# Merging 104 candidates instead of 192 in a top-32 scan, with its test on GpSimd, fills on VectorE and new orders

## The chip, the cores and the metric

The kernel runs on one core of a Trainium2 chip. The metric is the time of one execution in microseconds of the device, the median of several runs. Three runs of the kernel before gave 5827.73, 5835.18 and 5836.25 us.

## The reference

Input x is 16 batches of 256 rows of 128 columns; a context has 1601 rows for each batch. Four stages follow each other, each added to x through a gate: cross attention with 16 heads of 8 columns, a top-2 mixture of eight experts, a cross attention that keeps the 32 best keys of each query, and self attention with a second mixture. The change is in the third:

```
def _L1_xattn_ref(query, key, value, Wq, bq, Wk, bk, Wv, bv, Wo, bo):
    HID, NH, TOPK = (128, 16, 32)
    ...
    scores = jnp.einsum('bhqd,bhkd->bhqk', q, k) / SCALE
    top_scores, top_idx = jax.lax.top_k(scores, eff_k)
    w = jax.nn.softmax(top_scores, axis=-1)
    top_v = jnp.take_along_axis(v[:, :, None, :, :], top_idx[..., None], axis=3)
    out = jnp.einsum('bhqk,bhqkd->bhqd', w, top_v)
```

## The kernel before

Work is cut into batches (16) and groups of four heads (64, four to a batch). A step has a name and a key; each engine has a list of names (`ORDER`), which stands for one round of about a batch, and a table of lags (`LAG`) that says by how many steps each name stays behind. The list is gone through 21 times, so steps of some five batches are under way at once. Every engine does its list strictly in order; semaphores hold it back where data is missing.

The steps the text speaks of:

- `x_in`, `ctx_in`, `ln_stats`, `ln_aggr`, `ln_pow` (GpSimd, L1277), `ln_scale` (L1019), `ln_turn`, `w_k`, `w_q`: a batch is loaded, normalized, multiplied by weights. `split` (GpSimd, L1288 to L1295) cuts projected keys and queries into three bf16 parts, SP stores them in HBM (L1359) and loads them again, stacked, as `k_scan` and `k_att`.
- First scan (layer 0): `n0` multiplies scores on TensorE (L586) into one of two `score` banks, `n0_max` reduces them on VectorE into `part` (L1031).
- Second scan (layer 1): `c1` on TensorE (L601) fills one of the two `wide` buffers, `c1_out` on ScalarE (L886) copies them to `s`, four buffers of 128 queries x 1601 scores. Such a tile is one head's 128 queries; there are 512, 32 to a batch. `rank` on VectorE takes tile n and, between its searches, merges tile n - 1: it comes in four parts. The finding part (L933) takes the eight best of each of 24 pieces of 66 or 67 columns. The merging part (L949 to L978) takes the best 32 of the 192 candidates: four searches of eight, and between them three replacements of what was found by a very small number.
- The result is wrong only where a piece held more than seven of the best 32. So `eighth` is the largest of the 24 eighth values (L961), and `flag` tells whether it beats the 32nd (L978). For each pair of tiles `flag` on TensorE sums these flags over the queries (L768), `check` on VectorE reduces the sum (L1067), reads it into a register and, if it isn't zero, searches both tiles again over all 1601 columns (L1079, L1082). `c1_out` reuses a buffer of `s` only after the check of the tile four back. `least` (L1095 to L1106) makes the threshold of each query from its best and its 32nd value.
- Attention: `s_0`, `s_1`, `s_z` fill a `wide` buffer (L627, L639), ScalarE takes the exponential (L905), `pv` multiplies by the values (L673). For layer 1 ScalarE first marks what lies below the threshold (`cut`, L895), and `cut_add` (L649) adds it in place. `u_turn`, `o_norm`, `o_turn`, `o_proj`, `x_add` end a layer.
- All products that aren't in `wide`, `score` or `att` share one bank, `small`, which each user claims from the one before.

At the start GpSimd fills every buffer whose rows beyond the stacked ones must be zero or one (L1257 to L1265), and its first `ln_pow` and `split` come behind that.

## Time and profile before

| what | value |
|---|---|
| median of three runs | 5835.18 us |
| the profiled execution | 5828.82 us |
| its span, first to last instruction | 5826.2 us |
| TensorE, VectorE, ScalarE, GpSimd busy | 4721, 4724, 4048, 866 us |
| mean granted TensorE clock | 0.923 |
| HBM traffic | 56 GB/s over the span |

Busy times are the union of an engine's instructions. Of a matmul the end is modelled, so a busy TensorE is not one at its peak. VectorE's instructions overlap: each is recorded longer than the distance to the next one's start. In a row of a wait the engine that is named last held the other back.

### The profile page before, as it was taken

What the parts mean: (1) busy time and instruction counts of PE and PEld (TensorE: products, weight loads), DVE (VectorE), ACT (ScalarE), POOL (GpSimd) and SP (SyncE); (2) the same over time, 40 slices, a digit from 0 to 9 for tenths busy, and PEclk for the clock granted to TensorE, in tenths of its full rate; (3) what the DMA queues carried; (4) which work ended last, traced back from release to release, by engine and by line L of the source; (5) the groups of instructions that cost most, each with busy time, mean ns of one, the idle gap of its engine ahead of it and who ended that gap; (6) DMA issues with size and microseconds to landing.
All of it is one profiled execution on the core that took longest, in us unless ns stands there. A gap on an engine that the chain in (4) does not pass through costs nothing. (4 is left out here: it accounts for less than half of the span.)

```text
span 5826.2 us, 109134 instructions
## 1 busy us (share of the span) xinstructions
PE 4721.2 (81%) x34222; PEld 2250.7 (39%) x34758; DVE 4723.8 (81%) x23731; ACT 4047.7 (69%) x5196; POOL 866.3 (15%) x1650
## 2 busy tenths in 40 slices
PE   4878679898787989788788988887898788988666
PEld 1434234343343435334343534434353343434222
DVE  3468888888888888888888888888888888877773
ACT  1447667878586787768668787876878587786654
POOL 4211111111110111111111111111111111010000
PEclk7889889999899999999999999999999899998777
DMA  4322221312222222222212222221222222121110
GB/s 108 81 64 56 58 57 50 75 46 73 50 62 54 54 66 52 68 60 55 61 48 71 57 68 64 60 71 40 68 52 70 54 51 56 49 51 26 28 28 18
DMA packets 356330, 332.19 MB, mean 57 GB/s; under 512 B 102073, under 2 KB 313148, under 8 KB 355710
## 3 DMA queue, kind: packets, MB, share of 16 engines
q1 hardware_dynamic: 355710, 324.84, 22.6%
q8 instruction: 277, 4.54, 0.3%
q14 instruction: 343, 2.81, 0.2%
HBM read 217.54 MB, written 107.13 MB: 56 GB/s over the span
## 5 line engine op out<-in xcount | busy, mean ns | idle before, releaser
L933 DVE MAX8 cand<-s 128x8 f32<-128x67 f32 (+1 forms) x12288 | 2084.9, 216 | 235.3 <-ACT s L886 139.1
L905 ACT ACTIVATE prob<-wide 128x1024 f32<-128x1024 f32 (+1 forms) x1792 | 1765.7, 1024 | 380.9 <-PE wide L627 169.5
L1031 DVE TENSOR_REDUCE part<-score 128x1 f32<-128x512 f32 (+1 forms) x2048 | 1122.3, 565 | 429.2 <-PE score L586 286.2
L627 PE MATMUL wide<-q,k_att 128*128 128x256 bf16 (+1 forms) x6656 | 1027.8, 282 | 251.3 <-ACT prob L905 149.4
L673 PE MATMUL att<-prob,v 128*9 128x256 f32 (+1 forms) x14336 | 1118.2, 391 | 48.8 <-ACT prob L905 16.0
L886 ACT ACTIVATE s<-wide 128x1024 f32<-128x1024 f32 (+1 forms) x1024 | 827.4, 840 | 421.0 <-PE wide L601 290.0
L895 ACT ACTIVATE below<-wide 128x1024 bf16<-128x1024 f32 (+1 forms) x832 | 835.4, 1027 | 117.4 <-PE wide L627 110.7
L627 PEld LDWEIGHTS wide<-q,k_att 128*128 128x128 bf16 (+1 forms) x6656 | 563.0, 101 | 763.9 <-ACT prob L905 393.5
L586 PE MATMUL score<-k_scan,q 128*128 128x512 bf16 (+1 forms) x1724 | 560.6, 342 | 338.7 <-DVE part L1031 295.1
L601 PE MATMUL wide<-k_scan,q 128*128 128x512 bf16 (+1 forms) x1981 | 528.6, 356 | 71.3 <-ACT prob L905 33.6
L649 PE MATMUL wide<-below,minus_ident 128*128 128x512 bf16 (+1 forms) x1519 | 469.1, 392 | 101.6 <-ACT below L895 71.0
L586 PEld LDWEIGHTS score<-k_scan,q 128*128 128x128 bf16 x2048 | 199.0, 99 | 713.6 <-DVE part L1031 380.4
L673 PEld LDWEIGHTS att<-prob,v 128*9 128x9 f32 (+1 forms) x14336 | 227.1, 89 | 505.7 <-issue 395.3
L1304 POOL CAST shift<-minus 8x128 bf16<-8x128 f32 x192 | 54.0, 281 | 2114.8 <-issue 1886.0
L866 ACT ACTIVATE hid<-wide,b 128x256 f32<-128x256 f32 x512 | 200.5, 474 | 216.7 <-PE wide L715 216.5
L1288 POOL CAST split_b<-split_f 128x256 bf16<-128x256 f32 (+2 forms) x192 | 91.6, 477 | 1541.0 <-issue 860.3
L728 PE MATMUL small<-w,hid 128*128 128x128 f32 x2048 | 298.5, 289 | 0.0
L601 PEld LDWEIGHTS wide<-k_scan,q 128*128 128x128 bf16 x2048 | 153.2, 100 | 344.3 <-ACT s L886 125.8
L715 PE MATMUL wide<-v_xnT,w 128*128 128x256 f32 x1024 | 263.6, 403 | 23.0 <-ACT hid L866 17.0
L728 PEld LDWEIGHTS small<-w,hid 128*128 128x128 f32 x2048 | 249.5, 192 | 31.1 <-issue 0.4
L649 PEld LDWEIGHTS wide<-below,minus_ident 128*128 128x128 bf16 (+1 forms) x1664 | 113.9, 100 | 327.3 <-ACT below L895 275.9
L1277 POOL TENSOR_TENSOR rstd<-rstd,half 128x2 f32<-128x2 f32 x64 | 44.3, 693 | 1203.0 <-DVE rstd L1010 1201.8
(165 smaller groups left out, 5744.8 us busy)
## 6 DMA issues: line engine op xcount, KB each, us to landing
k_scan<-k_stack SPq DMA_DIRECT2D x512, 150.1 KB, 2.7
k_stack<-split_b SPq DMA_DIRECT2D x576, 128.0 KB, 2.5
k_att<-k_stack SPq DMA_DIRECT2D x384, 192.0 KB, 3.3
ctxT<-in_ctx_dram SPq DMA_DIRECT2D x32, 800.5 KB, 4.6
q_stack<-split_b SPq DMA_DIRECT2D x192, 64.0 KB, 2.1
q<-q_stack SPq DMA_DIRECT2D x128, 96.0 KB
self_stack<-split_b SPq DMA_DIRECT2D x192, 64.0 KB, 2.1
k_self<-self_stack SPq DMA_DIRECT2D x64, 96.0 KB
```

What stands on the lines that cost most here:

```text
L586: tensor.matmul(score[i % 2][:, 0:wd], m.q[0][g % QBUF[0]][:, hh, qt * P:(qt + 1) * P], m.k_scan[0][(HG * g + hh) % 2][:, a0:a0 + wd], sta ...
L601: r = tensor.matmul(ps[:, n0:n1], m.q[1][g % QBUF[1]][:, hh, qt * P:(qt + 1) * P], m.k_scan[1][(HG * g + hh) % 2][:, a0 + n0:a0 + n1], sta ...
L627: r = tensor.matmul(ps[0:kc, j * S:(j + 1) * S], m.k_att[kn % 3][:, j, c0:c0 + kc], rows[:, j, :], start=(j % 2 == 0), stop=(l == 0), skip ...
L649: r = tensor.matmul(ps[0:kc, x:x + BANK], m.minus_ident[0:kc, 0:kc], m.below[n % 2][0:kc, x:x + BANK], start=False, stop=True, skip_group_ ...
L673: r = tensor.matmul(att[32 * j:32 * j + HD + 1, 0:S], v[0:kc, c, j0 * HG + j, :], m.prob[n % 3][0:kc, j * S:(j + 1) * S], start=(c == 0), ...
L715: r = tensor.matmul(ps[:, k * S:(k + 1) * S], m.w_1[:, e, k * P:(k + 1) * P], m.xnT["v"][:, :], start=True, stop=True)
L728: r = tensor.matmul(ps[:, t * D:(t + 1) * D], hid[:, k, t * P:(t + 1) * P], m.w_2[:, e, k, :], start=False, stop=(k == PT - 1))
L886: scalar.activation(m.s[tile % 4][:, a0:a0 + wd], ps[:, 0:wd], ACT.Copy).then_inc(sem["wide_done"], 1)
L895: scalar.activation(m.below[n % 2][0:kc, :], ps[0:kc, :], ACT.Relu, scale=-STEEP).then_inc(sem["cut_done"], 1)
L905: scalar.activation(pr[0:kc, :], ps[0:kc, :], ACT.Exp, scale=SCALE).then_inc(sem["wide_done"], 1)
L933: i = vector.max(cand[:, c, :], s[:, KCUT[c]:KCUT[c + 1]])
L1031: vector.tensor_reduce(m.part[:, QT * hh + qt, c:c + 1], score[i % 2][:, 0:wd], AX.X, ALU.max).then_inc(sem["score_max"], 1)
```

## The change

It has five parts.

1. A buffer of candidates is now 8 + 192 columns wide and ordered by rank: first eight free columns, then the first values of all 24 pieces, then the second, and so on. Columns 8 to 103 are the four best of each piece, 104 to 199 the lower four. One search takes the best eight of the lower 96 into the free columns; the merge's searches and replacements run over columns 0 to 103. There are three such buffers and not two.
2. The result may be wrong where an eighth value of a piece, or the eighth of the lower ones, beats the 32nd. Both are compared on GpSimd, as a step `mark` with two operations per tile that write 25 flags in bf16; the product of `flag` has 50 columns, and `check` reduces 50.
3. In a part of `rank` three finding searches stand before each of two merging instructions, where two stood before each of up to three.
4. The fills of zeros and ones are done by VectorE before its first step.
5. `ORDER` and `LAG` of all engines are other tables.

```diff
-        "rank": 482, "n0_max": 257, "n0_all": 9, "o_norm.1": 17, "ln_scale.w": 1, "check": 61, "least": 16,
+        "rank": 491, "n0_max": 257, "n0_all": 9, "check": 62, "o_norm.1": 17, "least": 16, "x_add.1": 5,
...
-        m.cand = [sb(f"cand{n}", [P, KC, 8]) for n in range(2)]
-        m.left = sb("left", [P, KC, 8])
+        m.cand = [sb(f"cand{n}", [P, 8 + 8 * KC]) for n in range(3)]
+        m.left = sb("left", [P, 8 + 4 * KC])
-        m.eighth, m.flag = sb("eighth", [P, 1]), [sb(f"flag{n}", [P, QT]) for n in range(2)]
+        m.flag = sb("flag", [P, QT, KC + 1], BF16)
...
-                        q.wait_ge(ranked, 9 * (scan_tile(g, 2 * pair + 1) + 1))
-                        tensor.matmul(ps[0:1, 0:QT], m.ones_col[:, :], m.flag[(HG * g + pair) % 2][:, :],
+                        q.wait_ge(sem["marked"], after("mark", scan_tile(g, 2 * pair + 1)))
+                        tensor.matmul(ps[0:1, 0:QT * (KC + 1)], m.ones_col[:, :], flat(m.flag),
...
-                        if tile >= 2 and c == 0:
-                            q.wait_ge(ranked, 9 * (tile - 1))
-                        i = vector.max(cand[:, c, :], s[:, KCUT[c]:KCUT[c + 1]])
+                        if tile >= 3 and c == 0:
+                            q.wait_ge(ranked, 8 * (tile - 2))
+                            q.wait_ge(sem["marked"], after("mark", tile - 3))
+                        i = vector.max(cand[:, :, c], s[:, KCUT[c]:KCUT[c + 1]])
...
+                    upper, lower, left = cand[:, 0:8 + 4 * KC], cand[:, 8 + 4 * KC:], m.left[:, :]
+                    n, done = tile % 8, 8 * tile
                     best = [ends[:, n, 0, :], m.top[:, 0, :], m.top[:, 1, :], ends[:, n, 1, :]]
                     if part == 0:
                         q.wait_ge(cand_done, 4 * (tile + 1))
-                        q.wait_ge(ranked, done)
+                        vector.max(cand[:, 0:8], lower).then_inc(ranked, 1)
+                        yield
+                        q.wait_ge(ranked, done + 1)
                         if tile >= 16:
                             q.wait_ge(sem["least_done"], after("least", tile // 8 - 2))
+                        vector.max(best[0], upper).then_inc(ranked, 1)
+                        yield
                     else:
+                        q.wait_ge(ranked, done + 2 * part)
+                        vector.match_replace(left, best[part - 1], upper if part == 1 else left, NEG).then_inc(ranked, 1)
                         yield
+                        q.wait_ge(ranked, done + 2 * part + 1)
+                        vector.max(best[part], left).then_inc(ranked, 1)
                         yield
...
+                        for blank in (*m.q[0], *m.k_scan[0], *m.q[1], *m.k_scan[1]):
+                            vector.memset(blank[:, :] if len(blank.shape) == 2 else flat(blank), 0.0)
+                        for blank in (*m.k_att, *(x for pair in m.kq_self for x in pair)):
+                            i = vector.memset(flat(blank), 0.0)
+                        i.then_inc(blanked, 1)
+                        q.wait_ge(blanked, 1)
+                        for blank in (*m.k_att, *(x for x, _ in m.kq_self)):
+                            i = vector.memset(blank[32:ROWX, :, :], 1.0)
+                        i.then_inc(blanked, 1)
...
-                        for n in range(9):
-                            if n % 3 < 2:
+                        for n in range(8):
+                            if n % 4 < 3:
                                 next(finds, None)
                             else:
                                 next(merges, None)
...
-                        vector.tensor_reduce(m.many[:, :], small[0:1, 0:QT], AX.X, ALU.max).then_inc(sem["checked"], 1)
+                        vector.tensor_reduce(m.many[:, :], small[0:1, 0:QT * (KC + 1)], AX.X, ALU.max).then_inc(sem["checked"], 1)
...
+                    elif name == "mark":
+                        tile, = key
+                        cand = m.cand[tile % 3]
+                        flags, kth = m.flag, m.ends[tile // 8 % 2][:, tile % 8, 1, 7:8]
+                        q.wait_ge(ranked, 8 * (tile + 1))
+                        if tile >= 2:
+                            q.wait_ge(sem["small_full"], after("flag", (tile - 2) // 8, (tile - 2) % 8 // QT))
+                        gpsimd.tensor_scalar(flags[:, tile % QT, 0:KC], cand[:, 8 + 7 * KC:], kth, None,
+                                             ALU.is_gt).then_inc(sem["marked"], 1)
+                        gpsimd.tensor_scalar(flags[:, tile % QT, KC:KC + 1], cand[:, 7:8], kth, None,
+                                             ALU.is_gt).then_inc(sem["marked"], 1)
```

How instructions stand now, at three places. First VectorE in the middle of the program, from the last search of the merge of a pair's second tile (`ends<-left`) to that pair's check (`many`); the pair is the second of group 34. Before:

```order
L973 MAX ends<-left 128x8
L933 MAX cand<-s 128x8 x2
L978 TENSOR_TENSOR flag<-eighth,ends 128x1
...
L1216 SCALAR_TENSOR_TENSOR v_acc<-small,v_one,v_acc 128x128 x2
L933 MAX cand<-s 128x8 x2
L956 MAX top<-left 128x8
L933 MAX cand<-s 128x8 x2
L959 MATCH_REPLACE left<-top,left 128x192
L933 MAX cand<-s 128x8 x2
L961 TENSOR_REDUCE eighth<-cand 128x1
L1031 TENSOR_REDUCE part<-score 128x1 x2
L1067 TENSOR_REDUCE many<-small 1x1
```

And now:

```order
L1028 TENSOR_REDUCE part<-score 128x1
L1044 TENSOR_REDUCE mx<-score 128x2
L942 MAX cand<-s 128x8 x3
L964 MATCH_REPLACE left<-top,left 128x104
L942 MAX cand<-s 128x8 x3
L967 MAX ends<-left 128x8
L1064 TENSOR_REDUCE many<-small 1x1
L1066 TENSOR_LOAD many
```

The check has moved from two parts of a scan behind the merge to directly behind it. Over the middle 128 checks 2.8 parts of `rank` and 7.4 steps in all stood between the two in the mean; now it is 0.9 and 2.7, and in 8 of the 128 nothing stands between.

Second VectorE at the start of the program. Before:

```order
L984 MEMSET u 128x256
L1000 BN_STATS stats<-x 128x6 x2
L1007 BN_AGGR mv<-stats 128x2 x2
L1010 TENSOR_SCALAR rstd<-mv 128x2
L1019 TENSOR_SCALAR xn<-x,mv,rstd 128x128 x2
```

And now, where the widths are those of 32-bit words for the zeros of all but `k_scan`:

```order
L974 MEMSET q_2 128x512
L974 MEMSET k_scan_0 128x1601
L974 MEMSET k_scan_1 128x1601
L976 MEMSET k_att 128x1024 x3
L976 MEMSET k_self 128x512
L976 MEMSET q_self 128x512
L976 MEMSET k_self 128x512
L976 MEMSET q_self 128x512
L980 MEMSET k_att 19x2048 x3
L980 MEMSET k_self 19x1024 x2
L997 BN_STATS stats<-x 128x6 x2
```

All in all 22,276 columns of fills stand ahead of the first statistics.

Third GpSimd in the middle of the program, around the split of the last 65 columns of a projection. Before:

```order
L1288 CAST split_b<-split_f 128x65
L1290 TENSOR_TENSOR split_f<-split_f,split_b 128x65
L1293 CAST split_b<-split_f 128x65
L1295 TENSOR_TENSOR split_b<-split_f,split_b 128x65
L1304 CAST shift<-minus 8x128
L1306 TENSOR_TENSOR res<-minus,shift 8x128
```

And now:

```order
L1284 CAST split_b<-split_f 128x65
L1286 TENSOR_TENSOR split_f<-split_f,split_b 128x65
L1289 CAST split_b<-split_f 128x65
L1291 TENSOR_TENSOR split_b<-split_f,split_b 128x65
L1271 TENSOR_SCALAR flag<-cand,ends 128x24
L1273 TENSOR_SCALAR flag<-cand,ends 128x1
```

The marks stand in the same queue as splits and shifts and wait for whatever is in front.

## Rows read from the trace of the kernel before

**Rows 1.** The page, part 1: busy us, share of the span and instructions.
```profile
PE 4721.2 (81%) x34222; PEld 2250.7 (39%) x34758; DVE 4723.8 (81%) x23731; ACT 4047.7 (69%) x5196; POOL 866.3 (15%) x1650
```
**Rows 2.** Busy time by stretch: start:end, length, engines, granted clock, DMA share, GB/s.
```profile
787.00:1077.00 290.00, 234.35 (x1697) 116.05 (x1723) 253.19 (x1200) 200.94 (x265) 49.45 (x95) 0.93 0.24 57
3472.00:3798.00 326.00, 284.77 (x2142) 137.98 (x2172) 281.05 (x1474) 252.98 (x326) 51.53 (x100) 0.98 0.25 63
5586.00:5713.00 127.00, 81.47 (x546) 28.44 (x555) 91.14 (x561) 79.64 (x95) 8.43 (x24) 0.77 0.09 20
```
**Rows 3.** The last addition into x of two neighbouring batches, with their starts.
```profile
L1153 DVE SCALAR_TENSOR_TENSOR x<-z_acc,gates,x x2: 485/486/486, 3471.8 to 3797.9; 128x256 f32<-128x256 f32 x2
```
**Rows 4.** Waits from 3472 to 3798 us: total, times, longest.
```profile
DVE part L1031 <- PE score L586: 12.9, 16, 1.4
DVE many L1067 <- PE small L768: 2.6, 4, 1.2
```
```profile
PE wide L627 <- ACT prob L905: 9.5, 21, 1.0
PE score L586 <- DVE part L1031: 5.8, 9, 1.6
```
**Rows 5.** Timeline of VectorE, merging: start, duration, line, operation, count.
```profile
658.97 0.34 DVE L949 MAX8 ends<-cand 128x8 f32<-128x192 f32 x1
659.23 0.34 DVE L933 MAX8 cand<-s 128x8 f32<-128x67 f32 x2
659.49 0.07 DVE L952 MATCH_VALUE_LOAD left<-ends,cand 128x8 f32 x1
...
661.44 0.17 DVE L961 TENSOR_REDUCE eighth<-cand 128x1 f32<-128x24 f32 x1
661.53 0.34 DVE L933 MAX8 cand<-s 128x8 f32<-128x67 f32 x2
...
663.68 0.14 DVE L978 TENSOR_TENSOR flag<-eighth,ends 128x1 f32<-128x1 f32 x1
663.74 0.34 DVE L933 MAX8 cand<-s 128x8 f32<-128x66 f32 x2
```
**Rows 6.** VectorE by form (busy us, mean ns), and the flag line (minimum, median, maximum ns).
```profile
L978 DVE TENSOR_TENSOR flag<-eighth,ends 128x1 f32<-128x1 f32 x512 | 87.3, 170 | 0.0
L1082 DVE MAX8 ends<-s 128x8 f32<-128x1601 f32 x32 | 58.5, 1829 | 5.9 <-DVE many L1067 5.1
L1067 DVE TENSOR_REDUCE many<-small 1x1 int32<-1x2 f32 x256 | 35.6, 139 | 76.9 <-PE small L768 75.9
```
```profile
L978 DVE TENSOR_TENSOR flag<-eighth,ends x512: 132/143/1143, 382.9 to 5704.2; 128x1 f32<-128x1 f32 x171
```
**Rows 7.** GpSimd by form: one operation of a split, a small cast, the smallest fill.
```profile
L1295 POOL TENSOR_TENSOR split_b<-split_f,split_b 128x512 bf16<-128x512 f32 x96 | 111.2, 1159 | 7.7
L1309 POOL CAST shift<-res 8x128 bf16<-8x128 f32 x192 | 54.0, 281 | 12.3
L1444 POOL MEMSET const-float32-1.0<- 128x1 f32 x1 | 0.1, 98 | 0.0
```
**Rows 8.** The start: timeline rows of each engine, and busy times and DMA from 35 to 40 us.
```profile
0.86 0.27 DVE L984 MEMSET u<- 128x256 f32 x1 [0.86 <-PEq L1444]
44.35 1.95 DVE L1019 TENSOR_SCALAR xn<-x,mv,rstd 128x128 f32<-128x128 f32 x2 [23.83 <-POOL rstd L1277]
```
```profile
27.96 0.51 SPq L1324 DMA_DIRECT2D w<-in_L_ffn_W_dram  x1
48.15 7.71 SPq L1359 DMA_DIRECT2D k_stack<-split_b  x12
```
```profile
48.74 0.58 PE L541 MATMUL small<-w_oT,b_v 128*1 128x128 f32 x2
...
74.30 1.04 PE L586 MATMUL score<-k_scan,q 128*128 128x512 bf16 x2 [19.17 <-DMA k_scan<-k_stack]
```
```profile
35.00:40.00 5.00, 0.00 (x0) 0.00 (x0) 0.00 (x0) 0.00 (x0) 4.79 (x5) 0.50 0.00 0
```

More of the change, by code:

```diff
@@ L73 @@
     v_add=("v_added", 1), z_add=("z_added", 8), b_o_add=("b_o_done", 1), zero_u=("u_zero", 1),
-    ln_pow=("pow_done", 1), split=("split_done", 4), shift=("shift_done", 4),
+    ln_pow=("pow_done", 1), mark=("marked", 2), split=("split_done", 4), shift=("shift_done", 4),
 )
@@ L139 @@
     pool="""
-        shift.0 shift.1 split.w_k.0*2 ln_pow.z split.z_qk*2 ln_pow.v split.w_q shift.0 split.w_k.0 shift.1 shift.2
-        ln_pow.u shift.2 shift.0 split.u_q shift.1 split.w_k.0 shift.2 split.w_k.1 shift.2 shift.0 split.w_k.1*3
-        shift.1 ln_pow.w""",
+        mark shift.0 split.w_k.1 mark*4 shift.1 ln_pow.z mark*2 split.z_qk*2 mark ln_pow.v mark*2 shift.0 split.w_k.0
+        mark*2 shift.2 shift.1 ln_pow.w mark*3 split.w_k.0 mark split.w_q ln_pow.u mark shift.2 shift.0 mark
@@ L143 @@
+        split.w_k.0 split.u_q mark shift.2 mark shift.1 mark split.w_k.0 mark*4 shift.2 mark shift.0 split.w_k.1
+        mark*2 shift.1 mark split.w_k.1 mark*2 split.w_k.1 mark""",
     sp="""
-        q_in.1 k_scan.1 rows_out.0 rows_in.0 ctx_in.0 k_scan.0 k_att.0 k_att.1 k_scan.0 k_scan.1 rows_out.1 k_att.1*2
-        q_in.0 rows_in.1 split_out.w_k.0*2 k_scan.0 k_scan.1 k_att.1 k_att.0 k_scan.0 k_scan.1 k_att.0
-        split_out.z_qk*2 k_att.0 q_in.1 kq_in*2 split_out.w_q k_scan.1 rows_out.0 rows_in.0 split_out.w_k.0 k_scan.0
@@ L176 @@
     pool={
-        "shift.0": 9, "shift.1": 16, "split.w_k.0": 4, "ln_pow.z": 5, "split.z_qk": 10, "ln_pow.v": 3, "split.w_q": 1,
-        "shift.2": 20, "ln_pow.u": 3, "split.u_q": 3, "split.w_k.1": 8, "ln_pow.w": 0},
-    sp={
[3 rows of a table removed]
-        "split_out.w_k.1": 8, "x_out": 5, "x_in": 0},
+        "mark": 124, "shift.0": 9, "split.w_k.1": 9, "shift.1": 16, "ln_pow.z": 5, "split.z_qk": 10, "ln_pow.v": 3,
+        "split.w_k.0": 4, "shift.2": 20, "ln_pow.w": 1, "split.w_q": 1, "ln_pow.u": 3, "split.u_q": 3},
@@ L251, in streams @@
     of("rank", "rank", [(n, part) for n in range(QT * HG * NG + 1) for part in range(4)])
+    of("mark", "mark", [(n,) for n in range(QT * HG * NG)])
     for name in ("flag", "check"):
@@ L970, in merge @@
                         yield
                     else:
-                        q.wait_ge(ranked, done + 7)
-                        vector.max(best[3], left).then_inc(ranked, 1)
+                        q.wait_ge(ranked, done + 2 * part)
+                        vector.match_replace(left, best[part - 1], upper if part == 1 else left, NEG).then_inc(ranked, 1)
                         yield
-                        q.wait_ge(ranked, done + 8)
-                        if tile >= 4:
-                            q.wait_ge(sem["small_full"], after("flag", (tile - 4) // 8, (tile - 4) % 8 // QT))
@@ L978, in merge @@
-                        vector.tensor_tensor(m.flag[tile // QT % 2][:, tile % QT:tile % QT + 1], m.eighth[:, :],
-                                             ends[:, n, 1, 7:8], ALU.is_gt).then_inc(ranked, 1)
+                        q.wait_ge(ranked, done + 2 * part + 1)
+                        vector.max(best[part], left).then_inc(ranked, 1)
                         yield
```

216 lines of the change are left out of this document (94 added, 122 removed), and 6 rows, old and new, of the table sp.

## The prediction

> **What bounds the kernel now.** I read the page's busy shares first, then the steady stretch, then who waits for whom in it. The page has TensorE and VectorE level at 81% of the span, with ScalarE at 69% and GpSimd at 15% [rows 1]. Averages over the ramp hide the stage that counts. The last addition into x of a batch tells the pace: in a batch in which no scan is repeated it comes every 326.1 us [rows 3]. In exactly that stretch TensorE is busy 284.8 us, VectorE 281.1 and ScalarE 253.0 [rows 2]: two engines level at 87%, a third at 78%. No DMA matters there (0.25 of its engines busy). So this is not one bottleneck but three engines in fixed orders that lock into each other. The wait rows say how: VectorE's largest wait is for scores of TensorE, 12.9 us, and TensorE's are for ScalarE's `prob` (9.5 us on that one row) and for VectorE's `part` (5.8) [rows 4]. VectorE is idle 326.1 - 281.1 = 45 us in a batch, TensorE 41 us.
>
> **Part 1, the merges.** An instruction's mean hides what it costs, since VectorE's instructions overlap; the step from one start to the next does not. A search of 192 candidates starts at 658.97 and the next instruction at 659.23: 0.26 us. Two searches of a 67-column piece take 659.23 to 659.49, 0.13 each [rows 5]. The slope is (259 - 130) / 125 = 1.03 ns per column, so 104 columns cost 130 + 37 x 1.03 = 168 ns, and 96 cost 160. Before, a tile has seven passes over 192 (four searches, three replacements); each falls by 91 ns, together 0.64 us. Gone are the reduction of the eighths (661.44 to 661.53, 0.09 us) and the flag's comparison (663.68 to 663.74, 0.06 us, and now and then a stall: its median is 143 ns, its mean 170 and its longest 1143 [rows 6], so some 0.03 more). New is the search of the 96 lower candidates, 0.16. Net 0.64 + 0.09 + 0.06 + 0.03 - 0.16 = 0.66 us per tile. The loads of the eight values stay. The cost of the scattered store (eight values 24 columns apart) is in no row; I take it as nothing, from a search that puts out 8 values whatever it reads, and as the bad bound 8 cycles more per search, which at 1.03 ns is 24 x 8 = 198 ns per tile, a third of the gain.
>
> The check now reduces 50 columns where it reduced 2 [rows 6]: 48 x 1.03 = 0.05 us, 16 times a batch. A batch has 32 tiles: VectorE is relieved of 32 x 0.66 - 0.8 = 20.3 us, and in 512 tiles of 325 us.
>
> **How much of that reaches the end.** TensorE's work does not change (the flag product is small either way), so its 284.8 us stay. If the whole 20.3 us arrived, the batch would be 306 us and TensorE busy 93% of it; no stretch of the trace has it above 88%. The lower bound is what TensorE's own idle time owes to VectorE: 5.8 us for `part` [rows 4] and 5.9 in five smaller rows (`xn`, `mx`, `o`), together 11.7 us. The rest of its idle time is ScalarE's, whose work stays. Between 11.7 and 20.3 I take 14, nearer to the lower end, since that already asks for 91% of TensorE. VectorE would be at 84% then, and TensorE alone is late next. I count 14 batches at this gain (the stage from 787 us has VectorE at 87% too, TensorE at 81% [rows 2]): 196 us. In the last two batches VectorE is less busy, at the end 72% [rows 2], and waits for ScalarE's copies: half of 20.3 each, 20 us.
>
> **Part 2, repeats of a scan.** A repeat is 14 passes over 1601 columns at 1.8 us, 26 us in a batch; the row has 32 first or last searches of that width, two per tile, so 16 tiles in 8 pairs [rows 6]. The new rule also repeats when the eighth of the lower candidates beats the 32nd value. I worked both rules out on the reference's inputs: the same 8 pairs of 256 are marked, and no row has more than 5 of its best 32 among the lower candidates where 8 would be needed. Cost nothing, and nothing covers for it.
>
> **Part 3, the test on GpSimd.** Two comparisons a tile, 24 columns and 1. No such row exists here. From below stands a GpSimd fill of one column, 0.1 us; from above a cast on 8 x 128 at 281 ns [rows 7]. I take 0.25 each, nearer to the cast, which also reads. That is 16 us a batch on an engine that works 51.5 of 326 us [rows 2], so its time is free. What is not free is the chain. Before, the flag came from VectorE itself; now it goes last search, semaphore, two comparisons, TensorE's product, check: 0.5 for the comparisons, some 0.4 for the product and up to 0.3 for hand-overs, 1.2 us. Between the last search of a pair and its check stood 7.4 of VectorE's steps in the mean, 2.8 of them parts of a scan; now 2.7, of them 0.9 parts. A part takes about 1.1 us, so the cover is mostly still longer than 1.2; but in one check of 16 nothing at all stands between (the first place shown under the change), and in one a single short addition. That is 1.2 + 0.8 = 2 us a batch. GpSimd does its queue in order, and a mark may stand behind a split, which is four operations and some 3.5 us, the two long ones 1.16 each [rows 7]. Behind a waiting check on VectorE stand the searches of the next tile and `n0_max`, for which TensorE's scores wait. Before, the checks waited 2.6 us a batch [rows 4], so I charge 1 us more, 16 us in all.
>
> What speaks against the move is contention. The flag comparison's own row shows it: 143 ns as a rule, 1143 at worst when GpSimd was at work [rows 6]. The Trainium skill (SBUF — State Buffer, section SBUF: two separate sides) has one pair of ports that a GpSimd operation and a VectorE operation with two SBUF inputs hold for the whole instruction, the other being blocked. By that rule 1024 more GpSimd operations block VectorE's remaining two-input steps, some 40 a batch; at 0.25 us and GpSimd's 5% more occupancy that is under 1 us a batch, and the comparison that suffered most is the one removed. The sum is the same within its range.
>
> **Part 4, the start.** GpSimd fills until 43.5 us and makes the first `rstd` behind that, and only then can VectorE scale the first x (44.35), and SP store the first split (48.15), though SP's queue was through with the weights at 28.5 and nothing lands any more from 35 on, the weights included [rows 8]. TensorE's first score follows at 74.3. Now VectorE fills: 256 columns took 272 ns [rows 8], so 1.06 ns a column; 22,300 columns (zeros written as 32-bit words where the count allows, as the built program has it) are 23.7 us, and VectorE is free at 24.6. Then come 1.8 us of statistics and the power, so the first x is scaled at 26.8, 17.6 us sooner. SP's store can come 19.6 us sooner, and the bias product that waits for all weights can come by 35 at worst against 48.7 [rows 8], 13.7 us. So 14 to 17 us, and 10 if VectorE's fills had to wait for the 7 us of fills that GpSimd keeps. I take 15. The Trainium skill (VectorE: DVE Perf Modes, section Zero memsets can be issued as uint32) gives one cycle per element, 23.2 us for the same columns; the row and the rule agree, and the widths here come from it.
>
> **Part 5, the orders.** The second scan lags 4 half-tiles more and the attention of layer 1 by 7 of 52 chunks. The last step of a batch comes five rounds after its first in both, so there are 16 + 5 = 21 rounds in both; what leaves the ramp is added at the tail; I take nothing for it, within 10 us.
>
> **Sum.** The profiled execution took 5828.8 us; 5828.8 - 196 - 20 + 16 - 15 = 5614. The median of the runs is 6 us above that execution, so 5620.
>
> **Rivals.**
> *All of it arrives* (the new order lets TensorE reach 93%): 20.3 x 16 + 15 = 340 less, 5495. For it: the part of the wait rows that names ScalarE is itself a loop through the two wide buffers, which a new order can loosen. Against it: no stretch above 88%.
> *TensorE holds at its 88%*: the batch becomes 284.8 / 0.88 = 323.6 and 14 batches give 35; with the start and 10 at the tail 5775. The wait rows of ScalarE for TensorE speak for it.
> *The test becomes the new wait, slower than before*: place, the check on VectorE. The gain without it is 231 us over 256 checks, 0.9 us each. If marks come behind splits (3.5 us) where the cover is one part and one `n0_max`, 1.7 us, each check stalls by 1.2 us more: 307 us, and the time is 5829 - 231 + 307 + 6 = 5911. It decides from 0.9 us per check. Against it: GpSimd works 16% of a batch [rows 2], so few marks should find it busy.
> *Nothing moves*: the new order loses in ScalarE's loop what VectorE gains, 5835.
>
> **How the numbers follow.** The forecast (5530 to 5700) has 0.52, all of it 0.14, TensorE holds (5700 to 5820) 0.18, nothing 0.05, the test as new wait 0.11. Faster by over 0.2% is 0.52 + 0.14 + 0.18 = 0.84, the same 0.05, slower 0.11; 0.2%, 12 us, is about what a measurement of this kernel can tell from no change. The range leaves out the slower case and the lower half of the second, 0.18 in all, and so takes in the case in which nothing moves: 5490 to 5840.
>
> **What would show it.** A batch without a repeat near 312 us, with TensorE at about 285 and VectorE at about 261 busy: right. Searches over 104 columns that start 0.168 us before the next, else part 1 is off. The first score at 57 to 64 us, else part 4. VectorE's waits of `many` for the product near 4 us a batch; 15 or more would be the slower rival. A batch of 320 or more with few check waits would be TensorE's limit. A ninth pair scanned again would make part 2 wrong.

## The result, and the profile after

The changed kernel takes 5451.2 us (median of 4, 5441.8 to 5462.4) against 5831.5 for the kernel before on the same chip: a ratio of 0.934, interval 0.933 to 0.936. It is 380 us faster. The forecast was 5620 and the range ended at 5490: the sign was right, and the size missed by nearly a factor of two (215 us of gain forecast, 380 measured). The time lies below even the rival in which everything arrives, 5495.

The page of the changed kernel, part 1 (busy us, share of the span, instructions), answers to [rows 1]:

```profile
span 5460.3 us, 110204 instructions
...
PE 4684.1 (86%) x34502; PEld 2229.0 (41%) x34502; DVE 4361.7 (80%) x23240; ACT 4036.6 (74%) x5196; POOL 1154.4 (21%) x2648
```

VectorE works 362 us less, TensorE hardly less, and the span is 366 us shorter. TensorE's share rises from 81% to 86%. The same by stretch, as in [rows 2] (start:end, length, busy us of TensorE, weight loads, VectorE, ScalarE, GpSimd, granted clock, DMA share, GB/s), for the first full stage, a batch without a repeat, and the end:

```profile
787.00:1024.00 237.00, 199.13 (x1469) 98.31 (x1469) 198.47 (x967) 172.26 (x227) 49.35 (x114) 0.92 0.21 53
3270.00:3571.00 301.00, 280.15 (x2164) 135.72 (x2156) 257.21 (x1442) 252.16 (x326) 71.56 (x164) 1.00 0.27 68
5336.00:5460.00 124.00, 79.91 (x393) 29.55 (x393) 27.40 (x87) 40.94 (x55) 12.06 (x29) 0.64 0.09 21
```

And the pace, the last addition into x of two neighbouring batches of the changed kernel, as in [rows 3]:

```profile
L1150 DVE SCALAR_TENSOR_TENSOR x<-z_acc,gates,x x2: 1262/1263/1264, 3270.3 to 3571.4; 128x256 f32<-128x256 f32 x2
```

The batch takes 301 us, where it took 326. VectorE is busy 257.2 us in it (281.1 before), ScalarE unchanged. TensorE, whose work the change leaves alone, is busy 280.2 of 301 us: 93%, with an idle time of 21 us where it had 41. A part of that is the clock: its mean grant is 1.00 in this stage where it was 0.98, and the same work takes 4.6 us less. Over the whole run the mean grant is 0.936 where it was 0.923, and TensorE's busy time falls by 37 us, so as an estimate from these busy times the clock accounts for a tenth of the 366 us at most.

The 366 us between the two profiled executions lie in three places. Up to the last addition of the first batch (1077 us before, 1024 after) 53, of which 18 are gained by the first score. In the 12 batches behind it, 1077 to 5158 before and 1024 to 4835 after, 4081 against 3811 us: 270, or 22.5 a batch. In the rest 43. Six of these 12 batches have no repeat in either kernel; they took 326.3 us in the mean before and 302.5 now.

Who waits for whom in that batch of the changed kernel (engine, what, line, who is waited for: us in total, times, longest), as in [rows 4]:

```profile
PE wide L657 <- ACT below L903: 4.0, 12, 0.5
PE wide L609 <- ACT prob L913: 2.9, 8, 0.5
PE score L594 <- DVE part L1028: 2.1, 4, 0.7
PE wide L635 <- ACT prob L913: 2.0, 6, 0.5
PE wide L635 <- ACT s L894: 1.9, 4, 0.8
```
```profile
DVE v_acc L1213 <- PE small L736: 9.6, 5, 4.3
DVE part L1028 <- DVEq L1082: 8.5, 11, 0.9
DVE part L1028 <- PE score L594: 6.3, 12, 1.1
DVE many L1064 <- PE small L776: 6.0, 7, 2.5
DVE cand L942 <- ACT s L894: 3.8, 2, 3.3
```
```profile
ACT s L894 <- PE wide L609: 2.9, 7, 0.6
```

Two rows of the kernel before, from its 3472 to 3798 us, that [rows 4] don't show:

```profile
DVE v_acc L1216 <- PE small L728: 2.6, 3, 1.7
ACT s L886 <- PE wide L601: 17.0, 24, 3.2
```

TensorE's wait for `prob` at the products of the attention (`wide` of 128 x 256) was 9.5 us and is 2.0; its wait for `part` was 5.8 and is 2.1. ScalarE's wait for the second scan's products was 17.0 and is 2.9. Loops between TensorE and ScalarE are looser, in which VectorE has no part: over all rows of the batch TensorE waits for ScalarE 15.8 us where it waited 23.8. That is more than relief of VectorE, and the experiments have to say what it is. VectorE's own waits moved rather than fell: for scores 12.9 has become 6.3, but for the expert layer's products (`v_acc`) 2.6 has become 9.6, and at the checks (`many`) 2.6 has become 6.0. Over all rows it waits for TensorE 25.0 us where it waited 19.9.

### The profile page after: what moved, and what is told of

Same layout as the page of the kernel before. It is cut to its first block and busy times, and to the rows that moved or that the text cites. A ratio compares the mean times of both kernels' runs of the same rounds, so it can differ in the third digit from the quotient of the medians.

```text
span 5460.3 us, 110204 instructions
## 1 busy us (share of the span) xinstructions
PE 4684.1 (86%) x34502; PEld 2229.0 (41%) x34502; DVE 4361.7 (80%) x23240; ACT 4036.6 (74%) x5196; POOL 1154.4 (21%) x2648
## 5 line engine op out<-in xcount | busy, mean ns | idle before, releaser
L942 DVE MAX8 cand<-s 128x8 f32<-128x67 f32 (+1 forms) x12288 | 1988.3, 222 | 116.8 <-ACT s L894 67.5
L894 ACT ACTIVATE s<-wide 128x1024 f32<-128x1024 f32 (+1 forms) x1024 | 843.1, 845 | 309.6 <-DVEq L1082 174.5
L903 ACT ACTIVATE below<-wide 128x1024 bf16<-128x1024 f32 (+1 forms) x832 | 828.2, 1024 | 131.6 <-PE wide L635 123.5
L594 PE MATMUL score<-k_scan,q 128*128 128x512 bf16 (+1 forms) x2048 | 666.3, 349 | 220.9 <-DVE part L1028 178.7
L635 PEld LDWEIGHTS wide<-q,k_att 128*128 128x128 bf16 (+1 forms) x6656 | 583.3, 101 | 562.5 <-ACT s L894 149.5
L1271 POOL TENSOR_SCALAR flag<-cand,ends 128x24 bf16<-128x24 f32 x512 | 178.6, 349 | 2494.4 <-DVE ends L967 2243.5
L657 PE MATMUL wide<-below,minus_ident 128*128 128x512 bf16 (+1 forms) x1664 | 504.5, 386 | 97.2 <-ACT below L903 86.2
L967 DVE MAX8 top<-left 128x8 f32<-128x104 f32 x1024 | 257.9, 252 | 0.1
L964 DVE MATCH_REPLACE8 left<-top,left 128x104 f32<-128x104 f32 x1024 | 257.7, 252 | 0.0
L723 PE MATMUL wide<-v_xnT,w 128*128 128x256 f32 x1024 | 239.7, 388 | 9.6 <-ACT prob L913 9.0
L1284 POOL CAST split_b<-split_f 128x512 bf16<-128x512 f32 (+2 forms) x192 | 91.7, 477 | 674.6 <-issue 649.1
```

The costliest lines, as they stand in the source:

```text
L594: tensor.matmul(score[i % 2][:, 0:wd], m.q[0][g % QBUF[0]][:, hh, qt * P:(qt + 1) * P], m.k_scan[0][(HG * g + hh) % 2][:, a0:a0 + wd], sta ...
L635: r = tensor.matmul(ps[0:kc, j * S:(j + 1) * S], m.k_att[kn % 3][:, j, c0:c0 + kc], rows[:, j, :], start=(j % 2 == 0), stop=(l == 0), skip ...
L657: r = tensor.matmul(ps[0:kc, x:x + BANK], m.minus_ident[0:kc, 0:kc], m.below[n % 2][0:kc, x:x + BANK], start=False, stop=True, skip_group_ ...
L894: scalar.activation(m.s[tile % 4][:, a0:a0 + wd], ps[:, 0:wd], ACT.Copy).then_inc(sem["wide_done"], 1)
L903: scalar.activation(m.below[n % 2][0:kc, :], ps[0:kc, :], ACT.Relu, scale=-STEEP).then_inc(sem["cut_done"], 1)
L942: i = vector.max(cand[:, :, c], s[:, KCUT[c]:KCUT[c + 1]])
```

## The experiments

Two theories. **A**: VectorE's relief carries the gain, and comes through at 100% because nothing else was late. **B**: the orders and lags dealt anew carry it, and the narrower merges are a smaller share. Beside them stand smaller questions: the fills, the price of the test on GpSimd, and how much one microsecond of an engine's work is worth in the end time.

### The narrower merge alone, in the old orders

The kernel before with the buffer by rank and merges over 104 columns. The fills stay on GpSimd, orders and lags stay, and the test is one comparison on VectorE; the one of the lower eighth is left out. The reduction of the eighths stays too. A tile is relieved of 0.48 us, 245 us in all.

```diff
-        m.left = sb("left", [P, KC, 8])
+        m.left = sb("left", [P, 8 + 4 * KC])
...
-                        i = vector.max(cand[:, c, :], s[:, KCUT[c]:KCUT[c + 1]])
+                        i = vector.max(cand[:, :, c], s[:, KCUT[c]:KCUT[c + 1]])
...
+                        vector.max(cand[:, 0:8], lower).then_inc(ranked, 1)
...
-                        vector.max(best[0], cand).then_inc(ranked, 1)
+                        vector.max(best[0], upper).then_inc(ranked, 1)
```

> The kernel before with its own orders, its fills on GpSimd and its test on VectorE, but with the candidates ordered by rank and the merge over 104 of them. It leaves out the comparison of the eighth of the lower candidates with the 32nd value, which marks nothing on these inputs. VectorE is relieved of 7 x 0.091 - 0.160 = 0.48 us per tile, 15.3 us a batch and 245 us in all, against 20.3 in the changed kernel. Theory A (VectorE's relief is what made the gain, the orders only carry it): at least two thirds of the relief arrive, 5831 - 165 to 245, so 5590 to 5665. Theory B (the new orders made it: TensorE's idle time is a matter of the order): less than a third arrives, 5750 or more.

Measured: 5779.6 us, ratio 0.991 (0.990 to 0.993), 52 us faster. Of 245 us of relief a fifth arrives. A batch of it without a repeat (windows, then waits by engine):

```profile
3436.00:3759.00 323.00, 288.60 (x2173) 137.74 (x2172) 267.17 (x1506) 252.70 (x326) 51.55 (x100) 0.98 0.26 63
```
```profile
DVE part L1033 <- PE score L586: 23.6, 30, 2.1
...
PE wide L627 <- ACT prob L905: 8.5, 18, 1.0
...
ACT hid L866 <- PE wide L715: 14.5, 7, 4.0
ACT s L886 <- PE wide L601: 13.7, 20, 3.2
```

VectorE is busy 14 us less than in [rows 2] and waits 10.7 us more for scores (23.6 against 12.9 in [rows 4]): the relief turns into waiting. The batch falls by 3 us only, and so do the six batches without a repeat in the mean, 323.0 us against 326.3. Theory A falls as the cause of the whole.

### The new orders with the test on VectorE

The changed kernel with both comparisons on VectorE, right behind the last search of a tile; the marks leave GpSimd's list, every other order stays.

```diff
+                        if part == 3:
...
+                            q.wait_ge(ranked, done + 8)
+                            vector.tensor_scalar(flags[:, tile % QT, 0:KC], cand[:, 8 + 7 * KC:], kth, None,
+                                                 ALU.is_gt).then_inc(ranked, 1)
+                            vector.tensor_scalar(flags[:, tile % QT, KC:KC + 1], cand[:, 7:8], kth, None,
+                                                 ALU.is_gt).then_inc(ranked, 1)
...
-                    elif name == "mark":
```

> The changed kernel with the two comparisons of a tile done by VectorE directly behind the tile's last search, in place of GpSimd; all orders else the same. VectorE gets 0.09 + 0.06 + about 0.15 us of waiting for its own last search, 0.3 us x 32 = 10 us a batch, which at the slope of the added searches (60 us for 10.2 a batch) costs 60 us. The chain to the check loses GpSimd's two operations of 0.35 and 0.25 us and a hand-over, about 0.7 us per check; by the slope of the fourfold marks (262 us for some 1.9 us more per tile) that gives back 90 us. If the move to GpSimd was worth something, the time is over 5470; if the chain costs more than VectorE's time, it is 5400 to 5440.

Measured: 5495.5 us, ratio 0.943 (0.941 to 0.944); the changed kernel beside it on the same chip:

> The changed kernel itself, on the same chip as the run with the test on VectorE, to compare with: 5451 within 15 us.

Measured: 5450.8, ratio 0.935 (0.934 to 0.936). The test on GpSimd is worth 45 us. VectorE's timeline in the kernel with the test on VectorE:

```profile
2969.95 0.25 DVE L964 MAX8 ends<-left 128x8 f32<-128x104 f32 x1
2970.23 0.24 DVE L970 TENSOR_SCALAR flag<-cand,ends 128x24 bf16<-128x24 f32 x1
2970.38 0.21 DVE L972 TENSOR_SCALAR flag<-cand,ends 128x1 bf16<-128x1 f32 x1
2970.51 0.68 DVE L1034 TENSOR_REDUCE part<-score 128x1 f32<-128x512 f32 x1
```

The two comparisons take 0.15 and 0.12 us from start to start. The first also waits for the last search, whose value it compares with: 0.28 us pass from that search's start where such a search takes 0.17 otherwise, 0.12 us more in the mean of all tiles. Together that is 0.39 us a tile, some 200 us in all. On GpSimd VectorE is rid of it, and only the longer chain costs. Where the expectation puts the chain's price above the comparisons', it had the balance the wrong way round.

The kernel has a second use, since its batch does the same work as that of the experiment before. Its windows and waits:

```profile
2966.00:3270.00 304.00, 276.67 (x2130) 135.59 (x2164) 268.08 (x1506) 252.31 (x326) 51.88 (x101) 1.00 0.28 67
```
```profile
PE wide L633 <- ACT prob L911: 2.1, 7, 0.5
...
DVE part L1034 <- PE score L592: 1.5, 5, 0.6
...
ACT s L892 <- PE wide L607: 2.9, 7, 0.6
```

Both have 1506 instructions on VectorE, busy 267.2 and 268.1 us, ScalarE 252.7 and 252.3, GpSimd 51.6 and 51.9, and yet one batch takes 323 and the other 304. In the whole they differ by 5779.6 - 5495.5 = 284 us. Of these the fills take 22 (below). The other 262 are the orders and lags, and with them what else the two kernels do not share: the third candidate buffer, the dealing of the parts of `rank` (three finds before each merging step), and the form of the test (two comparisons that write 25 flags, reduced over 50 columns, in place of the eighths' reduction and one comparison). A part of the 262 comes by way of the clock, whose mean grant is 1.00 in the one batch and 0.98 in the other; TensorE's busy time is 12 us shorter there, some of it because 43 products fewer are recorded. VectorE waits for scores 1.5 us and not 23.6; ScalarE waits for the second scan's products 2.9 us and not 13.7 (17.0 in the kernel before), and its wait for the expert layer's first products at `hid` (L866), 14.5 us, is no longer among its seven largest waits. TensorE's wait for `prob` at the products of the attention goes from 8.5 to 2.1. Theory B stands, for the orders, lags and dealing taken together.

### The new orders under added work

The changed kernel with two more searches over all 200 columns in each tile, 0.53 us per tile, 273 in all, which gives VectorE back most of what the change took from it.

```diff
+                        for k in range(2):
+                            vector.max(m.spare[:, k, :], cand[:, :])
                         vector.max(best[0], upper).then_inc(ranked, 1)
```

> The changed kernel with two more searches of 200 columns per tile on VectorE, whose results nobody reads: 2 x 0.267 us x 32 = 17 us a batch, 273 us in all, so VectorE has nearly the load of the kernel before in the new orders. Theory A (relief): the time goes back by nearly all of it, 5690 to 5730. Theory B (orders): the batch stays below 312 us and the time below 5600.

Measured: 5583.9, ratio 0.958 (0.956 to 0.959). The batch:

```profile
3332.00:3642.00 310.00, 286.52 (x2157) 137.85 (x2156) 273.02 (x1506) 252.54 (x326) 71.34 (x164) 0.98 0.27 66
```

With VectorE's load almost that of before (273.0 of 281.1 us in a batch) the kernel is still 247 us faster than before. Going down from here to the changed kernel, 273 us of relief bring 133, half; in the old orders a fifth came through. The orders and the relief are worth more together than apart. Of the 247 us the fills are 22, and VectorE still has 8 us a batch less than in the kernel before, whose worth is in the 247 as well. So divided from this end the orders are worth 225 us at most and the relief 133 at least.

### What one microsecond of each engine is worth

Small changes of load, in both kernels. Two searches over 96 columns more per tile (0.32 us, 164 in all); the edit of the kernel before, while the changed one searches its lower 96 columns:

```diff
+                        for k in range(2):
+                            vector.max(m.spare[:, k, :], cand[:, 0:96])
```

> The kernel before with two more searches of 96 candidates per tile on VectorE, whose results nobody reads: 2 x 0.160 x 32 = 10.2 us a batch, 164 us in all. If VectorE sets the pace of the kernel before, the time rises by 110 to 164 us (5940 to 5995); if its 45 us of idle time a batch are slack, by less than 50.

> The changed kernel with two more searches of 96 candidates per tile on VectorE: 10.2 us a batch, 164 us in all. If TensorE, at 93%, now sets the pace and VectorE at 85% has slack, the time rises by less than 60 us (below 5511). If VectorE still sets it, by 110 to 164 us.

Measured: 5901.4, ratio 1.010 (1.007 to 1.013), and 5510.8, ratio 0.944 (0.943 to 0.946). The addition costs 61 us in the kernel before and 60 in the changed one: 0.37 us per us in both. The changed kernel by itself was not run beside these on this chip, and each cost is known to some 15 us, so to 0.1 us per us.

Three products of 128 x 128 in float32 ahead of each product of the flags, 768 in all:

```diff
+                        for k in range(3):
+                            tensor.matmul(ps[:, k * P:(k + 1) * P], m.ident[:, :], m.ident[:, :], start=True, stop=True)
```

> The kernel before with three more 128 x 128 f32 products per flag product on TensorE, about 0.6 us x 16 = 10 us a batch, 155 us in all. If TensorE's work can be packed denser (93% in the changed kernel) and VectorE sets the pace, the time rises by less than 60 us. If TensorE is level with VectorE in setting the pace, as its busy time says, by 100 to 160.

> The changed kernel with three more 128 x 128 f32 products per flag product on TensorE, about 10 us a batch, 155 us in all. If TensorE now sets the pace, the time rises by 120 to 160 us (5570 to 5610). If it can still be packed denser, by less than 60.

Measured: 5992.7, ratio 1.027 (1.025 to 1.029), and 5619.9, ratio 0.963 (0.961 to 0.965): 152 to 161 and 160 to 169 us, by whether the comparison is with the kernel on the same chip or with its median elsewhere. The added work in the kernel before (TensorE by form):

```profile
L769 PE MATMUL small<-ident 128*128 128x128 f32 x1536 | 247.2, 301 | 43.0 <-DVE flag L980 21.8 <-DVE o L1127 21.2
```

These are 1536 records, two for each product. From start to start a record takes 0.149 us in the kernel before and 0.142 in the changed one, so the work added is 229 and 218 us, and 0.66 to 0.70 and 0.73 to 0.78 of it arrives. Where the expectation of the changed kernel without bias products (below) gives these products 0.142 us each and 109 us in all, it counts one record for a product; the 169 us are not more than the work but less. The products also stand in the chain from the last search to the check, so they lengthen that chain as well as TensorE's work, and the two can't be told apart here.

So the same question from the other side, with TensorE's work taken away. The products that add the bias of the expert layer's second matrix are left out (256, in 512 records of 0.207 us, 106 us in all), and with them that bias in what is computed.

```diff
-                            tensor.matmul(ps[:, t * D:(t + 1) * D], one[0], b_2[:, e * D:(e + 1) * D],
-                                          start=True, stop=False)
...
-                                                  m.w_2[:, e, k, :], start=False, stop=(k == PT - 1))
+                                                  m.w_2[:, e, k, :], start=(k == 0), stop=(k == PT - 1))
```

> The kernel before without the same bias products (left out of its output too), 106 us of TensorE in all. If TensorE set the pace of the kernel before too, the time falls by 80 to 110 us (5725 to 5755); if its 41 us of idle time a batch are slack that the order fixes elsewhere, by less than 50.

> The changed kernel without the bias products of the expert layer (32 per batch of 1 x 128 f32, 0.207 us each from start to next start): 6.6 us of TensorE a batch, 106 us in all. It leaves out that bias. The three products added before each flag product measured 0.142 us each, 109 us in all, but cost 169, since they also stood in the chain to the check; these don't. If TensorE's work sets the pace, the time falls by 80 to 110 us (5340 to 5370); if fixed chains do and TensorE has slack, by less than 50.

Measured: 5774.2, ratio 0.990 (0.988 to 0.991), and 5383.1, ratio 0.923 (0.921 to 0.925). 59 and 68 us less. But these two kernels do more of something else: without the bias other values reach the scan, and nine pairs are scanned again where [rows 6] have eight (36 first searches of 1601 columns for 32):

```profile
L1080 DVE MAX8 ends<-s 128x8 f32<-128x1601 f32 x36 | 65.8, 1829 | 7.0 <-DVE many L1065 6.0
L1077 DVE MAX8 ends<-s 128x8 f32<-128x1601 f32 x36 | 65.8, 1829 | 6.7 <-DVE many L1062 5.8
```

A batch with one pair scanned again takes 28 us longer than one without in the kernel before, and 30 in the changed one. With that added back, as an estimate, some 86 and 98 of the 106 us arrive. The batches without a repeat need no such estimate. One of each kernel, by the last additions into x:

```profile
L1151 DVE SCALAR_TENSOR_TENSOR x<-z_acc,gates,x x2: 484/484/484, 3393.2 to 3717.8; 128x256 f32<-128x256 f32 x2
L1148 DVE SCALAR_TENSOR_TENSOR x<-z_acc,gates,x x2: 1259/1260/1260, 3154.8 to 3450.4; 128x256 f32<-128x256 f32 x2
```

324.6 and 295.6 us. The mean of the batches without a repeat between the first and the thirteenth last addition (six in each kernel, seven without the bias) moves as follows, in us; they differ among themselves by 1 to 2.4 us:

| what is done to every batch | work, before / changed | kernel before (326.3) | changed kernel (302.5) |
|---|---|---|---|
| searches on VectorE added | +10.2 / +10.2 | +6.6 | +3.4 |
| products on TensorE added | +14.3 / +13.6 | +11.1 | +10.2 |
| bias products on TensorE left out | -6.6 / -6.6 | -3.4 | -6.8 |

In the kernel before no engine sets the pace by itself: about half of what is taken from TensorE comes back, and two thirds of what is added to VectorE is felt. In the changed kernel all of what is taken from TensorE comes back, and a third of what is added to VectorE is felt, so that TensorE, at 93%, comes close to setting the pace there. It is not shown to be TensorE's work alone: the bias products also stand in front of `v_acc`, for which VectorE waits 9.6 us a batch in the changed kernel. That 0.37 came out in both kernels over the whole run is the mean of unlike stretches.

### The fills

The changed kernel with all fills of zeros and ones on GpSimd again.

```diff
-                        for blank in (*m.q[0], *m.k_scan[0], *m.q[1], *m.k_scan[1]):
-                            vector.memset(blank[:, :] if len(blank.shape) == 2 else flat(blank), 0.0)
...
+                for blank in (*m.k_scan[0], *m.k_scan[1]):
+                    gpsimd.memset(blank[:, :], 0.0).then_inc(filled, 1)
```

> The changed kernel with the fills back on GpSimd, as before. If the start is worth what the first scores show (74.3 us before, 56.4 after), the time goes up by 18 us to 5469. If the new order of the first round hides it, by less than 8. The rival in which fills on VectorE cost something later gives no rise.

Measured: 5473.6, ratio 0.938 (0.937 to 0.940), 22 us more than the changed kernel. Its first transposition on TensorE waits for the scaled x until 48.8 us (timeline of this kernel):

```profile
48.80 0.69 PE L537 MATMUL small<-ident,xn 128*128 128x128 f32 x2 [34.39 <-DVE xn L1007]
```

### The test's chain made longer

Each of the two comparisons of a mark done four times, one behind the other.

```diff
+                        for again in range(4):
+                            if again:
+                                q.wait_ge(sem["marked"], before(name, *key) + 2 * again)
...
```

> The changed kernel with each tile's two comparisons on GpSimd done four times in a row, each pair waiting for the one before: some 2.5 us per tile instead of 0.6, all in front of TensorE's flag product. If the chain from merge to check is just covered, as the waits of the check for the product (6 us a batch) suggest, each check comes up to 1.9 us later for most pairs: 100 to 450 us more, 5550 to 5900. If the cover is ample, under 30 us more.

Measured: 5714.5, ratio 0.981 (0.979 to 0.983), 263 us more than the changed kernel. Three more pairs of comparisons lengthen a mark by 3 x 0.65 = 1.95 us at least, and a check comes 256 times: 1.0 us of each arrives. A late batch of it, in which some of the other stages' work has run out (316 instructions of ScalarE and not 326), and its waits:

```profile
4711.00:5025.00 314.00, 277.81 (x2118) 131.97 (x2116) 255.50 (x1434) 247.88 (x316) 116.33 (x335) 0.98 0.22 53
```
```profile
DVE many L1064 <- PE small L776: 20.0, 12, 3.3
...
PE small L776 <- POOL flag L1276: 15.3, 11, 3.0
```

The same batch takes 299.8 us in the changed kernel, and the six without a repeat take 318.2 in the mean against 302.5, again 1.0 us for each of 16 checks. GpSimd is busy 116 of 314 us, so it is its delay that costs and not its load. VectorE waits 20.0 us at the checks (6.0 in the changed kernel), TensorE 15.3 at the product in front of them, and what is queued behind it waits too. The cover under the chain is short: the forecast's slower rival was wrong in how late the marks come, not in that a late mark is paid for.

## Why the prediction missed

Four kernels in a row divide the gain: 5831 to 5780 by the narrower merge in the old orders, **52**; to 5496 by orders, lags, third buffer, dealing and form of the test, **262**, and by the fills, **22**; to 5451 by the test on GpSimd, **45**. Divided from the other end the shares shift, since relief is worth more in the new orders: at most 225 for the orders, at least 133 for VectorE's relief. The orders are the largest part in the first division; in the second they may be no larger than the relief, and no run settles it.

**What bounds the kernel** was read rightly: three engines in fixed orders that lock into each other. In the kernel before, a us of TensorE's work and one of VectorE's are both worth part of a us. What the forecast says comes next, TensorE alone, is borne out too: in the changed kernel's batches its work comes back in full.

**Part 1, the merges**, holds. VectorE's timeline in the changed kernel:

```profile
3299.73 0.49 DVE L942 MAX8 cand<-s 128x8 f32<-128x67 f32 x3
3300.12 0.25 DVE L955 MAX8 cand<-cand 128x8 f32<-128x96 f32 x1
3300.28 0.48 DVE L942 MAX8 cand<-s 128x8 f32<-128x67 f32 x3
3300.67 0.26 DVE L960 MAX8 ends<-cand 128x8 f32<-128x104 f32 x1
3300.84 0.68 DVE L1028 TENSOR_REDUCE part<-score 128x1 f32<-128x512 f32 x1
```

The search of 96 takes 3300.12 to 3300.28, 0.16 us, that of 104 takes 3300.67 to 3300.84, 0.17, and three pieces take 0.39, 0.13 each. These are the values of the sum, and the scattered store costs nothing. The relief came out at 23.9 us of busy time a batch where 20.3 were worked out.

**How much of that reaches the end is the step that failed.** It took 14 of 20.3 us a batch, because 14 asks for 91% of TensorE and no stretch of the trace had it above 88%; 22.5 came, with TensorE at 93%. It failed twice over, in opposite directions. For the relief alone 14 was far too much, and so was its lower bound of 11.7, the part of TensorE's idle time that is put down to VectorE: in the old orders 3 us a batch arrived of 15.3, and TensorE's wait for `part` went from 5.8 to 8.4. And the cap was no cap: the highest share seen was a property of the order in which the engines' work was dealt, not of TensorE. The rest of TensorE's idle time was taken as fixed because ScalarE's work stays; that work did stay (253.0 and 252.2 us), and TensorE's waits for it fell from 23.8 to 15.8. A deal in which VectorE does the same amount of work ran it at 277 of 304 us, 91%, and the final kernel at 93%.

**Part 5, the orders, is where the gain was missing.** They were costed at nothing within 10 us, from the count of rounds alone; they brought 262, or 225 at most by the other division. The two failures offset each other in part, so that the forecast stands nearer to the measured time than its terms do. The wait rows had the room for it on display: in [rows 4] 12.9 us of VectorE for scores and 9.5 of TensorE for `prob` stood in one batch, while every engine had 41 us or more of idle time, and ScalarE waited 17.0 us for the second scan's products. The forecast named this as the rival in which all arrives ("a loop through the two wide buffers, which a new order can loosen") and gave it 0.14, with a time that still counted only VectorE's relief. Which of the tables did it, or the lag of the second scan or the parts of `rank`, stays open: no kernel here changed them one by one. The third buffer can hardly be it, since with two of them the finding searches waited 0.5 us a batch for VectorE's own earlier steps and 10.6 for scores and register reads. That the longer lag lets TensorE deliver the second scan's products before ScalarE asks for them fits ScalarE's wait of 17.0 us that became 2.9, but is argued and not shown.

**Part 2, repeats**, holds: 8 pairs were scanned again in both.

**Part 3, the test**, was charged 16 us, against a credit (in part 1) for the reduction and comparison that fall away. The rows of the changed kernel, GpSimd by form (busy us, mean ns, idle before):

```profile
L1271 POOL TENSOR_SCALAR flag<-cand,ends 128x24 bf16<-128x24 f32 x512 | 178.6, 349 | 2494.4 <-DVE ends L967 2243.5 <-issue 154.3 <-PE small L622 61.9
L1273 POOL TENSOR_SCALAR flag<-cand,ends 128x1 bf16<-128x1 f32 x512 | 153.9, 301 | 0.0
```

They take 0.35 and 0.30 us, not 0.25, and the checks wait 6.0 us a batch, not 4; with the test on VectorE they wait 3.2. The charge was too small. As an estimate, the 200 us that the test takes of VectorE would be worth 74 to 98 at 0.37 to 0.49 us per us (the two additions in the changed kernel), and 45 came, so that the chain costs 29 to 53 us. The slower rival's threshold of 0.9 us per check came from a gain of 231; with 380 us of gain it lies higher, and the quadrupled marks, at 1.0 us per check, leave the kernel faster than before.

**Part 4, the start**, holds in its mechanism, with 22 us where the sum has 15. Timelines of VectorE, SP and TensorE in the changed kernel:

```profile
22.59 0.91 DVE L980 MEMSET k_self<- 19x1024 bf16 x1 [0.16 <-issue]
23.67 0.91 DVE L980 MEMSET k_self<- 19x1024 bf16 x1 [0.16 <-issue]
24.61 0.49 DVE L997 BATCH_NORM_STATS2 stats<-x 128x6 f32<-128x128 f32 x2
...
26.47 0.60 DVE L1016 TENSOR_SCALAR xn<-x,mv,rstd 128x128 f32<-128x128 f32 x2 [0.88 <-POOL rstd L1261]
```
```profile
28.52 9.38 SPq L1355 DMA_DIRECT2D k_stack<-split_b  x12
```
```profile
31.55 0.59 PE L549 MATMUL small<-w_oT,b_v 128*1 128x128 f32 x2 [1.18 <-DMA w<-in_L_ffn_W_dram]
...
56.45 1.03 PE L594 MATMUL score<-k_scan,q 128*128 128x512 bf16 x2 [18.11 <-DMA k_scan<-k_stack]
```

VectorE is free at 24.61 (24.6 worked out), x is scaled at 26.47 (the forecast's 26.8 should have been 26.4 by its own terms, 24.6 + 1.8), SP stores at 28.52 as soon as its weight loads are issued, and the first score comes at 56.45, 17.9 us sooner, just ahead of the 57 to 64 given. The fills undone cost 22 us.

**The tail** was 20 in the sum and 43 in the traces, the same error as in the batches.

## What to carry to other kernels

Where several engines run fixed orders and all sit between 75% and 90%, the highest share seen in a trace is no ceiling, and a new deal of the orders is a term of its own, possibly the largest. Bound it by the idle time that the orders cause, not by the count of rounds. Before trusting a relief of one engine, measure a slope, and measure it in the direction in which you want to go: in the old orders a us added to VectorE cost 0.6 us in a batch without a repeat, but of a us taken away 0.2 came back. And look at what the dummy change does to the rest of the program; leaving out a bias here brought a ninth pair to be scanned again, which hid a third of the gain.

## What the hardware showed beside

The last addition into x took 485 ns in every batch of the kernel before and takes about 1261 in 13 of the changed kernel's 16, where GpSimd works at a split at the same time (source row, then the timelines of GpSimd and VectorE around one of them):

```profile
L1150 DVE SCALAR_TENSOR_TENSOR x<-z_acc,gates,x x16: 485/1261/1265, 1023.5 to 5457.6; 128x256 f32<-128x256 f32 x16
```
```profile
3270.05 1.21 POOL L1286 TENSOR_TENSOR split_f<-split_f,split_b 128x512 f32<-128x512 f32 x1
3270.28 1.26 DVE L1150 SCALAR_TENSOR_TENSOR x<-z_acc,gates,x 128x256 f32<-128x256 f32 x1
```

VectorE's operation starts 0.23 us behind GpSimd's and ends 0.28 us behind it, at 3271.54 against 3271.26. The Trainium skill (SBUF — State Buffer, section SBUF: two separate sides) has the operation of VectorE with two SBUF inputs blocked for the whole of GpSimd's when that holds the pair of ports; the trace agrees. In the kernel with the test on VectorE the same addition meets a shorter operation of GpSimd, a cast of 0.69 us, takes 714 ns and again ends 0.28 us behind it. With 13 such additions it costs some 10 us of VectorE.

A fill of 1024 columns on VectorE is recorded with 0.91 us and one of 1601 with 1.39, some 0.87 ns a column where 1.06 were worked out from 256 columns. But from start to start the 1024 columns took 1.08 us (22.59 to 23.67), so 1.05 ns a column. The recorded length falls short of the step from one fill to the next, and it is the step that counts: all fills together took 23.4 us, from 1.17 to 24.61, against the prediction's 23.7.
